# Early narrow products with sides exchanged, output weights split sooner, and adapter tables with the chunk index innermost

## The chip, the cores and the metric

One NeuronCore of a Trainium2 chip runs the kernel. Its engines have a row each in the profile: TensorE (PE, with its weight loads as PEld), VectorE (DVE), ScalarE (ACT), GpSimd (POOL), and SyncE (SP), which here only issues DMAs. The metric is device microseconds of one execution, the median of several.

## What is computed

A stream x of 32 sequences x 64 tokens x 512 channels, float32, passes four residual layers:

```python
x = x + attention(x)      # paged cache, window 256, 8 query heads, 4 key heads of 64
x = x + x @ w1[subject]   # one of eight 64 x 64 matrices, applied along the tokens of a batch
x = x + x @ W_base.T + ((x @ Wt.T) @ A2[a].T @ B2[a].T) @ Wp.T * scale2[a]
x = x + x @ W3.T + (x @ A3[b].T @ B3[b].T) * scale3[b]
```

Keys and queries are normalised and rotated; new keys and values go into the cache before it is read. The adapters have rank 16; there are 4 in the third layer and 8 in the fourth.

## The kernel before

Each engine's program is written out by hand, with semaphores between them; what an engine does, it does in the order of its own list. A tile is two batches (128 tokens), so there are 16 tiles; a step k of the main loop is one batch of attention (32 steps).

**Before the loop.** TensorE makes keys and values of all 16 tiles (`key_tile`, two per `key_pair`), which VectorE rotates and SP stores to `newkv`. Then it makes `queries(0)`, and from weights alone the folded matrices: the last two layers are linear, so they become one dense matrix `wf` and rank-32 terms per adapter pair. First come two narrow products of 512 x 512 weights with 64 columns: `wpt` with `b2` (called up, to `upt`) and `wt` with `a2` (to `t2tab`). `turned` makes each as 16 products with 128 columns of weights and 64 moving columns. Then `ct`, the product `t3` (`turned` with 128 moving columns, to `t3tab`), `u2f`, `queries_t(0)`, `keys_t(0)`, and `combined` and `fold` between the first `scores`. What is needed in two parts, a float32r high part and the rest, is copied by ScalarE (`..._high`, `evac`) and subtracted on VectorE (`low`, `..._low`): queries' and output weights through three `stage` buffers (`split_high`, `split_low` on POOL for the first four, `wo_low` for the last four). `root` on POOL is the power -1/2 of the norms; the gathers of cache rows are on the same queue.

**Tables.** `t2tab` and `t3tab` go to DRAM (`ttab2`, `ttab3`), and `load_tile` on SP fetches for each tile the four that its adapters need into `tsel`. In `ranks`, `tsel` is the weights' side of eight products with 128 moving columns, once for the high and once for the low part of x2:

```python
last = mm(sbk[2][:, 0:128], tsel[t % 2][:, c].rearrange("p v r -> p (v r)"), x2_s[a][:, c, :],
```

**The loop.** TensorE's even step: `keys_t` (transposes of cached keys), `queries(t+1)`, `probs_t` 0 and 1 (transposes of probabilities), `scores` of the next batch, `probs_t` 2 and 3, `project` (attention's output), `values`. Odd step: `keys_t`, `mix` (layer two of the tile before), `queries_t(t+1)` (transposes of the rotated query), `probs_t` 0 and 1, `scores`, `probs_t` 2 and 3, `base` and `ranks` (layers three and four), `values`, `up`. Bank `gb` is shared by `queries`, `project`, `mix` and `base`/`up`, so `queries` waits until ScalarE (`out_ev`) has emptied it. VectorE's even step: `attn_low`, `query_first`, four `soft` (mask and maximum of scores), `query_sums`, `scale(n, 0)`, `residual`, `query_last`, `scale(n, 1)`. Three batches of `newkv` and cache rows are gathered ahead.

Of the kernel before, what the change touches and what calls it, by code (L numbers as in the profile page):

```python
# [7 lines left out]
NB, NT, D = 32, 64, 512  # L8
# [67 lines left out]
def build(nc, xt, xtok, kvrows, wkv, wq, wo, qs, ks, w1, wbn, wt, a2t, b2t, wpt, s2, w3, a3t, b3t, s3,  # L76
# [4 lines left out]
    with ctx:  # L81
# [11 lines left out]
        ttab2 = nc.dram_tensor("ttab2", [NE2, 128, C, 2 * RANK], f32).ap()  # L93
        ttab3 = nc.dram_tensor("ttab3", [NE3, 128, C, 2 * RANK], f32).ap()
# [14 lines left out]
        t2tab = sb("t2tab", [128, NE2, C, 2, RANK], f32r)  # L109
        t3tab = sb("t3tab", [128, NE3, C, 2, RANK], f32r)  # L110
# [79 lines left out]
        def early(name, shape, dt=f32):  # L190
# [26 lines left out]
        tsel = [sb(f"tsel{i}", [128, C, 4, 2 * RANK], f32r) for i in range(2)]  # L217
# [12 lines left out]
            wb_ident w3_ident split_hi split_lo wo_lo up_mm up_ev t2_mm t2_hi t2_ev t3_mm t3_hi t3_ev ct_mm ct_ev u2f_mm u2f_ev u2_stored  # L230
# [17 lines left out]
        PAIRS = TILES // 2  # L248
        FOLD_BANKS = [ob, gb, tb[1], ob]
# [20 lines left out]
        def _(sp):  # L270
# [39 lines left out]
            for i in range(PAIRS):  # L310
                key_x(2 * i + 4)
                if i == 5:
                    spread_rows()
                key_x(2 * i + 5)
                for dst, src, name in pieces[i * each:(i + 1) * each]:
                    sp.dma_start(dst, src).then_inc(S[name], 16)
                if i >= 1:
                    store_pair(i - 1)
                if i == 2:
                    sp.wait_ge(S["split_lo"], 1)  # L320
                    load_split(3)
            store_pair(PAIRS - 1)
            for k in range(C, 2 * C):
                sp.wait_ge(S["split_lo"], min(k - 2, C))
                after(sp, S["wo_lo"], k - 2 - C)
                load_split(k)
# [11 lines left out]
            def load_tile(t):  # L338

                i = t % 2  # L340
                after(sp, S["x1_ready"], t)
                sp.dma_start(xtok_s[:], xtok[t]).then_inc(S["l_xtok"], 16)
                after(sp, S["l1_mm"], t - 1)
                for u in range(2):
                    s = sp.value_load(subj_s[0:1, 2 * t + u:2 * t + u + 1], min_val=0, max_val=7)
                    h = slice(64 * u, 64 * u + 64)
                    sp.dma_start(w1i[i][h, h], wtab[bass.ds(s, 1)].rearrange("a c n -> (a c) n")).then_inc(l_w1[i], 16)
                after(sp, S["out_mm"], t - 1)
                for u in range(2):
                    a2 = sp.value_load(ad2_s[0:1, 2 * t + u:2 * t + u + 1], min_val=0, max_val=NE2 - 1)  # L350
                    a3 = sp.value_load(ad3_s[0:1, 2 * t + u:2 * t + u + 1], min_val=0, max_val=NE3 - 1)
                    a23 = sp.value_load(pair_s[0:1, 2 * t + u:2 * t + u + 1], min_val=0, max_val=NE2 * NE3 - 1)
                    for l, tab, a in ((0, ttab2, a2), (1, ttab3, a3)):
                        sp.dma_start(tsel[i][:, :, 2 * u + l].bitcast(f32),
                                     tab[bass.ds(a, 1)].rearrange("a p c r -> (a p) c r")).then_inc(l_sel[i], 16)
                    sp.dma_start(usel[i][64 * u:64 * u + 32, :],
                                 utab2[bass.ds(a23, 1)].rearrange("a h r n -> (a h r) n")).then_inc(l_sel[i], 16)
                    sp.dma_start(usel[i][64 * u + 32:64 * u + 64, :],
                                 utab3[bass.ds(a3, 1)].rearrange("a h r n -> (a h r) n")).then_inc(l_sel[i], 16)
# [13 lines left out]
            sp.dma_start(ttab2.rearrange("e p c r -> p e (c r)"), t2tab[:].bitcast(f32).rearrange("p e c h r -> p e (c h r)")).then_inc(S["u_stored"], 16)  # L373
            sp.wait_ge(S["t3_ev"], 1)
            sp.dma_start(ttab3.rearrange("e p c r -> p e (c r)"), t3tab[:].bitcast(f32).rearrange("p e c h r -> p e (c h r)")).then_inc(S["u_stored"], 16)
# [27 lines left out]
        def _(pool):  # L403
# [57 lines left out]
            gather(0, 0)  # L461
            gather(1, 0)
            root("k", 7, 0)
            gather(2, 0)
            root("k", 8, 0)
# [22 lines left out]
        def _(act):  # L488
# [50 lines left out]
            for i in range(4, 7):  # L539
                key_pair(i)  # L540
            xq_high(0)
# [7 lines left out]

            query_square(0)  # L550
            split_high(4)
            evac(upt[:], bank[4][:, 0:256].rearrange("p (c r) -> p c r", c=C).unsqueeze(2).to_broadcast([128, C, 2, 64]), "up_mm", "up_ev")
            split_high(5)
            split_high(6)
            evac(t2tab[:, :, :, 0].rearrange("p e c r -> p c e r"), bank[5][:, 0:256].rearrange("p (c e r) -> p c e r", c=C, e=NE2), "t2_mm", "t2_hi")
# [47 lines left out]
            split_high(7)  # L603
            evac(t3tab[:, :, :, 0].rearrange("p e c r -> p c e r"), tb[1][:].rearrange("p (c e r) -> p c e r", c=C, e=NE3), "t3_mm", "t3_hi")
# [6 lines left out]
            for j in range(3):  # L611
                fold_high(j)
# [3 lines left out]
            for k in range(NB):  # L616
                t, n = k // 2, k + 1
                if k % 2 == 0:
                    if t >= 1:
                        attn_high(t - 1)  # L620
                    if t >= 2:
                        out_ev(t - 2)
                    if k > 0:
                        keys_ev(n)
                        if t + 1 < TILES:
                            query_square(t + 1)
                    probs_ev(k, 0)
                    probs_ev(k, 1)
                    exps(n, 0)
                    probs_ev(k, 2)  # L630
                    probs_ev(k, 3)
                    exps(n, 1)
                    exps(n, 2)
                    exps(n, 3)
                else:
                    if n < NB:
                        keys_ev(n)
                    if t >= 1:
                        mixed_high(t - 1)
                    if t + 1 < TILES:  # L640
                        queries_ev(t + 1)
                    probs_ev(k, 0)
                    probs_ev(k, 1)
                    if n < NB:
                        exps(n, 0)
                    probs_ev(k, 2)
                    probs_ev(k, 3)
                    if n < NB:
                        exps(n, 1)
                        exps(n, 2)  # L650
                    if t + 2 < TILES:
                        xq_high(t + 2)
                    if n < NB:
                        exps(n, 3)
# [7 lines left out]
        def _(dve):  # L662
# [165 lines left out]
            def wo_low(k):  # L828
# [6 lines left out]
            query_sums(0)  # L835
            wo_low(4)
            wo_low(5)
            low(t2tab[:, :, :, 0].rearrange("p e c r -> p c e r"), t2tab[:, :, :, 1].rearrange("p e c r -> p c e r"),
                bank[5][:, 0:256].rearrange("p (c e r) -> p c e r", c=C, e=NE2), "t2_hi", 1, "t2_ev")
            query_last(0)  # L840
            wo_low(6)
            xq_low(1)
            wo_low(7)
            low(t3tab[:, :, :, 0].rearrange("p e c r -> p c e r"), t3tab[:, :, :, 1].rearrange("p e c r -> p c e r"),
# [36 lines left out]
            def ranks(t):  # L881
                dve.wait_ge(S["z_mm"], t + 1)
                V.tensor_tensor(zm, sbk[2][:, 0:128], con("same_batch"), ALU.mult).then_inc(S["z_ready"], 1)
# [15 lines left out]
            scale(0, 1)  # L899
            combine(2)  # L900
# [6 lines left out]
            for k in range(NB):  # L907
                t, n = k // 2, k + 1
                if k % 2 == 0:
                    if t >= 1:  # L910
                        attn_low(t - 1)
                        if t + 1 < TILES:
                            query_first(t + 1)
                    else:
                        query_last(1)
                    for g in range(G):
                        soft(n, g)
                    if 0 < t < TILES - 1:
                        query_sums(t + 1)
                    scale(n, 0)  # L920
                    if t >= 1:
                        residual(t - 1)
                    if 0 < t < TILES - 1:
                        query_last(t + 1)
# [21 lines left out]
        def _(pe):  # L946
# [33 lines left out]
            def queries_t(t):  # L980
                pe.wait_ge(S["q_rot"], t + 1)
                after(pe, S["z_ready"], t - 2)
# [33 lines left out]
            pe.wait_ge(S["split_lo"], C)  # L1016
            queries(0)

# [5 lines left out]

            pe.wait_ge(S["l_wpt"], 16 * C)
            pe.wait_ge(S["l_low"], 32)
            pe.wait_ge(S["rows_ready"], 1)
            turned(bank[4], wpt_s, b2_s, 64).then_inc(S["up_mm"], 1)
            pe.wait_ge(S["l_wt"], 16 * C)
            turned(bank[5], wt_s, a2_s, 64).then_inc(S["t2_mm"], 1)  # L1030
# [39 lines left out]
            def scores(b):  # L1070
                t, u = b // 2, b % 2
                pe.wait_ge(S["qt_ev"], t + 1)
                if u == 0:
                    after(pe, S["z_ready"], t - 2)
# [46 lines left out]
            def ranks(t, b):  # L1121
                pe.wait_ge(l_sel[t % 2], 128 * (t // 2 + 1))
                pe.wait_ge(S["x2_lo"], t + 1)
                after(pe, S["negs_ready"], min(4 * b + 3, 4 * NB))
                for a in range(2):
                    for c in range(C):
                        last = mm(sbk[2][:, 0:128], tsel[t % 2][:, c].rearrange("p v r -> p (v r)"), x2_s[a][:, c, :],  # L1127
# [19 lines left out]
            for k in range(NB):  # L1147
# [18 lines left out]
                else:  # L1166
                    if t >= 1:
                        mix(t - 1)
# [3 lines left out]
                    probs_t(k, 1)  # L1172
                    if n < NB:
# [69 lines left out]
```

## Time and profile before

| what | us |
|---|---|
| median of 3 runs | 474.25 (472.82 to 475.46) |
| the profiled execution: time | 475.29 |
| its span, first to last instruction | 473.4 |
| mean granted clock of TensorE | 0.993 |
| busy: PE, DVE, ACT, POOL | 448.3, 277.2, 225.1, 260.0 |

The span is what the trace covers. Matmuls overlap in the pipeline, so their start-to-start distance, not their duration, tells what one costs. In a timeline, a bracket at the end of a row says how long the engine had been idle before it and what ended that.

### The profile page before, as it was taken

To read this page: it belongs to the slowest core of one execution; us is meant where nothing else is said; L and a number is where in the kernel's file an instruction comes from. 1 tells how busy PE (TensorE), PEld (TensorE's weight loads), DVE (VectorE), ACT (ScalarE), POOL (GpSimd) and SP (SyncE) were. 2 spreads that over 40 slices of the span, in tenths; PEclk is the share of its full clock that TensorE was granted. 3 is DMA by queue.
4 is the path that set the end of the run, shared out by engine and by line. 5 is a ranking of instruction groups with operands and counts; after the bars stand their busy time and mean duration, and the time that the engine had idled before them with its cause. 6 is when DMAs were issued, how large, how long until landed. Compare 5 with 4: busy or idle time off the path is not lost.

```text
span 473.4 us, 9807 instructions
## 1 busy us (share of the span) xinstructions
PE 448.3 (95%) x2847; PEld 320.8 (68%) x2847; DVE 277.2 (59%) x801; ACT 225.1 (48%) x600; POOL 260.0 (55%) x240
## 2 busy tenths in 40 slices
PE   5999997999989999999999999999999999999985
PEld 1434436745668777777777787877777777778763
DVE  2998867453666656464847466655646484746411
ACT  1331211352845564555647465556455564746521
POOL 3468176833355656666666565565666666654000
PEclk9999998999989999999999999999999999999999
DMA  7669676664444555556464636455554646352220
GB/s 227 212 201 310 208 256 191 182 201 129 114 124 105 161 128 152 133 153 152 128 164 116 173 104 169 110 148 133 154 142 128 160 131 159 95 156 71 72 70 22
DMA packets 81402, 70.34 MB, mean 149 GB/s; under 512 B 51684, under 2 KB 57700, under 8 KB 81350
## 3 DMA queue, kind: packets, MB, share of 16 engines
q1 hardware_dynamic: 64688, 47.23, 35.3%
q0 software_dynamic: 15456, 22.08, 17.0%
q10 hardware_dynamic: 1206, 0.42, 0.4%
q8 instruction: 23, 0.38, 0.3%
q14 instruction: 29, 0.24, 0.2%
HBM read 79.66 MB, written 11.93 MB: 193 GB/s over the span
## 4 chain that ended last, share of the span: by engine, by line
PE 76%; DVE 7%; ACT 5%; issue 5%; POOL 3%; DMA 3%; SPq 0%; ACTq 0%; POOLq 0%; DVEq 0%
PE bank L957 29%; PE bank L1099 9%; PE bank L1081 9%; PE bank L1087 7%; PE bank L951 4%; PE bank L1133 4%; PE bank L1114 3%; PE bank L970 3%; PE bank L1127 3%; PE bank L1066 3%; ACT w_late L595 2%; ACT qt_s L585 2%; POOL windows L454 2%; DMA cst<-const_dram 2%; DMA stage<-wo_dram 1%
## 5 line engine op out<-in xcount | busy, mean ns | idle before, releaser
L454 POOL DMA_INDIRECT windows<-kvrows_dram,idx_all x96 | 97.1, 1011 | 76.9 <-PE bank L1099 56.4
L454 POOL DMA_INDIRECT windows<-newkv,idx_all x96 | 96.3, 1003 | 35.9 <-issue 28.9
L567 ACT ACTIVATE prob<-prob,negmax 128x336 f32<-128x336 f32 x128 | 72.5, 570 | 30.7 <-DVE negmax L857 30.7
L427 POOL TENSOR_TENSOR rstd<-ms,half 128x8 f32<-128x8 f32 x24 | 46.4, 1932 | 47.6 <-DVE ms L796 28.9
L970 PE MATMUL bank<-wkv_s,xt_s 128*128 128x512 f32 x128 | 60.3, 629 | 6.5 <-DMA wkv_s<-wkv_dram 5.8
L857 DVE CUSTOM_DVE_ANT_0 prob<-bank,mask 128x336 f32<-128x336 f32 x128 | 57.2, 503 | 15.0 <-PE bank L1081 13.8
L573 ACT ACTIVATE pt_s<-bank 112x384 f32<-112x384 f32 x128 | 55.1, 485 | 0.3 <-PE bank L1087 0.3
L1087 PE MATMUL bank<-cst,prob 128*112 128x128 f32 x384 | 54.3, 278 | 0.5 <-ACT pt_s L573 0.5
L1087 PEld LDWEIGHTS bank<-cst,prob 128*112 128x112 f32 x384 | 42.4, 134 | 17.8 <-issue 15.9
L970 PEld LDWEIGHTS bank<-wkv_s,xt_s 128*128 128x128 f32 x128 | 25.0, 200 | 39.5 <-issue 36.9
L1099 PE MATMUL bank<-pt_s,windows 112*64 112x128 f32 x768 | 49.4, 277 | 0.3 <-ACT pt_s L573 0.3
L789 DVE TENSOR_TENSOR t<-bank,qcos 128x512 f32<-128x512 f32 x16 | 11.1, 692 | 61.1 <-ACT sq L548 61.1
L1099 PEld LDWEIGHTS bank<-pt_s,windows 112*64 112x64 f32 x768 | 41.2, 137 | 7.7 <-issue 5.8
L1081 PE MATMUL bank<-kt_s,qt_s 64*128 64x336 f32 x256 | 44.8, 468 | 1.5 <-issue 0.2
L867 DVE TENSOR_SCALAR prob<-prob,rinv 128x336 f32<-128x336 f32 x128 | 44.9, 393 | 2.3
L561 ACT ACTIVATE kt_s<-bank 128x336 f32<-128x336 f32 x64 | 25.3, 449 | 27.5 <-PE bank L1066 27.5
L957 PE MATMUL bank<-wq_hi,xq_hi 128*128 128x512 f32 x64 | 28.0, 437 | 8.7 <-DVE xq_lo L823 6.1
L1081 PEld LDWEIGHTS bank<-kt_s,qt_s 64*128 64x128 f32 x256 | 22.1, 186 | 14.4 <-ACT qt_s L585 5.0
L548 ACT ACTIVATE sq<-bank 128x512 f32<-128x512 f32 x16 | 9.6, 597 | 46.7 <-PE bank L957 46.7
L957 PE MATMUL bank<-wf_hi,x_hi 128*128 128x512 f32 x64 | 26.6, 415 | 1.4 <-DVE x_lo L823 1.4
L957 PE MATMUL bank<-wo_hi,ot_hi 128*128 128x512 f32 x64 | 26.5, 414 | 0.8 <-ACT w_late L595 0.8
L1066 PEld LDWEIGHTS bank<-cst,windows 112*128 112x128 f32 x192 | 20.0, 141 | 10.3 <-issue 6.6
(171 smaller groups left out, 772.2 us busy)
## 6 DMA issues: line engine op xcount, KB each, us to landing
xt_s<-xt_dram SPq DMA_DIRECT2D x32, 256.0 KB, 3.3
mask<-masks_dram SPq DMA_DIRECT2D x32, 168.0 KB
newkv<-kvo SPq DMA_DIRECT2D x16, 256.0 KB, 3.8
stage<-xtok_dram SPq DMA_DIRECT2D x16, 256.0 KB, 2.5
tsel<-ttab SPq DMA_DIRECT2D x64, 64.0 KB
out_dram<-w_late SPq DMA_DIRECT2D x16, 256.0 KB, 4.4
stage<-utab SPq DMA_DIRECT2D x32, 64.0 KB
wbn_late<-utab SPq DMA_DIRECT2D x32, 64.0 KB
```

Source lines behind the costliest of these rows:

```text
L427: P.tensor_tensor(rstd[i][:], ms[:], half[:], ALU.pow).then_inc(S[w + "_rstd"], 1)
L454: P.indirect_dma_start(kv_s[b % 4][:, c, :], None, newkv if new else kvrows, bass.IndirectOffsetOnAxis(ap=idx_all[:, new * CH + c, b:b + 1 ...
L567: A.activation(pr, pr, ACT.Exp, bias=negmax[:, g:g + 1], scale=-1.0, accum_out=psum_p[b % 2][:, g:g + 1]).then_inc(S["exp_done"], 1)
L573: A.activation(pt_s[g][:], tb[g % 2][0:KP, 0:CH * 128].rearrange("p (c q) -> p c q", c=CH), ACT.Copy).then_inc(S["pt_ev"], 1)
L857: V.tensor_tensor_reduce(out=prob[b % 3][:, g, :], in0=sbk[g][:, 0:WK], in1=mask[b % 3][:], scale=-1.0 / 16, scalar=3.0e38, op0=ALU.add, o ...
L867: V.tensor_scalar(pr, pr, rinv[b % 2][:, g:g + 1], None, ALU.mult).then_inc(S["norm_done"], 1)
L957: last = mm(to, lhs(a, c), rhs(b, c), start=(c == 0 and a == b), stop=(c == C - 1 and a == 1 and not more))
L970: last = mm(to[:], xt_s[n % 4][:, c, :], wkv_s[:, c, :], start=(c == 0), stop=(c == C - 1))
L1066: last = nc.tensor.transpose(sbk[p][:, KP * c:KP * c + KP], kv_s[b % 4][:, c, 128 * p:128 * p + 128], ident[0:KP, 0:KP])
L1081: mm(sbk[g][:, 0:WK], qt_s[t % 2][r, cols], kt_s[b % 2][p][r, :], start=True, stop=True).then_inc(S["s_mm"], 1)
L1087: last = nc.tensor.transpose(tb[g % 2][0:KP, 128 * c:128 * c + 128], prob[b % 3][:, g, KP * c:KP * c + KP], ident)
L1099: last = mm(ob[64 * h:64 * h + 64, col:col + 128], kv_s[b % 4][:, c, 256 + 64 * g:320 + 64 * g], pt_s[g][:, c, :], start=(c == 0), stop=(c ...
```

## The change

- The two narrow products are made together ahead of `queries(0)`: the 64-column side becomes the weights and the 512 x 512 side moves, up's in the lower and t2's in the upper 64 partitions of bank 4. ScalarE copies the result to `lows`, and TensorE turns it with four transposes into bank 5.
- Splits 4 and 5 (output weights) go up between the last key pairs on ScalarE, and the loads 4, 5 and 6 on SP up among the key tiles' loads; split 7 goes down behind `fold_high(0)`. Root 7 on POOL comes one gather earlier, and root 8 too.
- In the loop `mix` and `mixed_high` go behind the first two `probs_t` and `probs_ev`; on VectorE `query_sums` follows `query_first`, and `query_last` goes ahead of `residual`.
- `ranks` writes bank 0 instead of bank 2 and waits for the maxima of the first score group rather than of three; the waits of `queries_t` and `scores` on `z_ready` go.
- `t2tab`, `t3tab`, their DRAM tables and `tsel` have the chunk of 128 model columns (4 of them) as innermost index.

```diff
-        t2tab = sb("t2tab", [128, NE2, C, 2, RANK], f32r)
-        t3tab = sb("t3tab", [128, NE3, C, 2, RANK], f32r)
+        t2tab = sb("t2tab", [128, NE2, 2, RANK, C], f32r)
+        t3tab = sb("t3tab", [128, NE3, 2, RANK, C], f32r)
...
-        tsel = [sb(f"tsel{i}", [128, C, 4, 2 * RANK], f32r) for i in range(2)]
+        tsel = [sb(f"tsel{i}", [128, 4, 2 * RANK, C], f32r) for i in range(2)]
...
+        lows = u2c[3]
+        low_t = bank[5][:].rearrange("p (c r) -> p c r", c=C)
...
-                if i == 2:
-                    sp.wait_ge(S["split_lo"], 1)
-                    load_split(3)
+                k = {2: 3, 3: 4, 4: 5, 6: 6}.get(i, 0)
+                if k:
+                    sp.wait_ge(S["split_lo"], k - 2)
+                    load_split(k)
             store_pair(PAIRS - 1)
-            for k in range(C, 2 * C):
-                sp.wait_ge(S["split_lo"], min(k - 2, C))
-                after(sp, S["wo_lo"], k - 2 - C)
-                load_split(k)
+            sp.wait_ge(S["wo_lo"], 1)
+            load_split(7)
...
-                        sp.dma_start(tsel[i][:, :, 2 * u + l].bitcast(f32),
-                                     tab[bass.ds(a, 1)].rearrange("a p c r -> (a p) c r")).then_inc(l_sel[i], 16)
+                        sp.dma_start(tsel[i][:, 2 * u + l].bitcast(f32),
+                                     tab[bass.ds(a, 1)].rearrange("a p r c -> (a p) r c")).then_inc(l_sel[i], 16)
...
             gather(0, 0)
+            root("k", 7, 0)
             gather(1, 0)
-            root("k", 7, 0)
+            root("k", 8, 0)
             gather(2, 0)
-            root("k", 8, 0)
             root("q", 1, 1)
...
                 key_pair(i)
+                if i > 4:
+                    split_high(i - 1)
             xq_high(0)
...
+            evac(lows, bank[4][:], "low_mm", "low_ev")
             query_square(0)
-            split_high(4)
-            evac(upt[:], bank[4][:, 0:256].rearrange("p (c r) -> p c r", c=C).unsqueeze(2).to_broadcast([128, C, 2, 64]), "up_mm", "up_ev")
-            split_high(5)
+            evac(upt[:], low_t[:, :, 0:64].unsqueeze(2).to_broadcast([128, C, 2, 64]), "low_t", "up_ev")
+            evac(t2tab[:, :, 0].rearrange("p e r c -> p c e r"), low_t[:, :, 64:128].rearrange("p c (e r) -> p c e r", e=NE2), "low_t", "t2_hi")
             split_high(6)
-            evac(t2tab[:, :, :, 0].rearrange("p e c r -> p c e r"), bank[5][:, 0:256].rearrange("p (c e r) -> p c e r", c=C, e=NE2), "t2_mm", "t2_hi")
...
-            for j in range(3):
+            fold_high(0)
+            split_high(7)
+            for j in range(1, 3):
                 fold_high(j)
...
-                    if t >= 1:
-                        mixed_high(t - 1)
                     if t + 1 < TILES:
                         queries_ev(t + 1)
                     probs_ev(k, 0)
                     probs_ev(k, 1)
+                    if t >= 1:
+                        mixed_high(t - 1)
...
                         if t + 1 < TILES:
                             query_first(t + 1)
+                            query_sums(t + 1)
...
+                    scale(n, 0)
                     if 0 < t < TILES - 1:
-                        query_sums(t + 1)
-                    scale(n, 0)
+                        query_last(t + 1)
                     if t >= 1:
                         residual(t - 1)
-                    if 0 < t < TILES - 1:
-                        query_last(t + 1)
                     scale(n, 1)
...
-            turned(bank[4], wpt_s, b2_s, 64).then_inc(S["up_mm"], 1)
-            pe.wait_ge(S["l_wt"], 16 * C)
-            turned(bank[5], wt_s, a2_s, 64).then_inc(S["t2_mm"], 1)
+            for c in range(C):
+                for h, r, w in ((0, b2_s, wpt_s), (1, a2_s, wt_s)):
+                    last = mm(bank[4][64 * h:64 * h + 64, :], r[:, c, :], w[:, c, :], start=(c == 0), stop=(c == C - 1))
+            last.then_inc(S["low_mm"], 1)
+            pe.wait_ge(S["split_lo"], C)
+            queries(0)
+            pe.wait_ge(S["low_ev"], 1)
+            for c in range(C):
+                last = nc.tensor.transpose(low_t[:, c, :], lows[:, 128 * c:128 * c + 128], ident)
+            last.then_inc(S["low_t"], 1)
...
-                        last = mm(sbk[2][:, 0:128], tsel[t % 2][:, c].rearrange("p v r -> p (v r)"), x2_s[a][:, c, :],
+                        last = mm(sbk[0][:, 0:128], tsel[t % 2][:].rearrange("p v r c -> p (v r) c")[:, :, c], x2_s[a][:, c, :],
...
-                    if t >= 1:
-                        mix(t - 1)
                     if t + 1 < TILES:
                         queries_t(t + 1)
                     probs_t(k, 0)
                     probs_t(k, 1)
+                    if t >= 1:
+                        mix(t - 1)
```

## Rows read from the trace of the kernel before

**Rows 1.** The page: TensorE's busy time, and the chain that ended last.

```profile
PE 448.3 (95%) x2847; PEld 320.8 (68%) x2847; DVE 277.2 (59%) x801; ACT 225.1 (48%) x600; POOL 260.0 (55%) x240
...
PE 76%; DVE 7%; ACT 5%; issue 5%; POOL 3%; DMA 3%; SPq 0%; ACTq 0%; POOLq 0%; DVEq 0%
```

**Rows 2.** Busy time in one tile's period; last columns: clock, DMA share, GB/s.

```profile
287.23:309.21 21.98, 21.70 (x158) 16.93 (x159) 12.97 (x40) 12.58 (x35) 13.97 (x13) 1.00 0.55 142
```

**Rows 3.** Waits from 155 to 440 us: total, times, longest.

```profile
PEld bank L1066 <- DMA windows<-newkv,idx_all: 3.3, 12, 0.3
...
PEld bank L1081 <- ACT qt_s L585: 4.3, 13, 0.3
...
PE bank L957 <- ACT w_late L595: 2.6, 13, 0.2
PEld bank L1081 <- issue: 2.3, 13, 0.2
```

**Rows 4.** TensorE's timeline before the loop: start, duration, line, form.

```profile
74.31 0.47 PE L957 MATMUL bank<-wq_hi,xq_hi 128*128 128x512 f32 x1 [3.92 <-DVE xq_lo L823]
...
78.72 3.68 PE L951 MATMUL bank<-b_s,wpt_late 128*128 128x64 f32 x32
...
85.81 1.06 PE L951 MATMUL bank<-upt,a_s 128*128 128x64 f32 x8
87.88 3.81 PE L951 MATMUL bank<-a_s,wbn_late 128*128 128x128 f32 x32 [1.01 <-DVE t2tab L823]
...
94.96 0.60 PE L986 MATMUL bank<-cst,qrot 128*128 128x128 f32 x4
```

**Rows 5.** One microsecond within `queries(0)`, columns as in rows 2.

```profile
75.00:76.00 1.00, 1.00 (x5) 0.71 (x4) 1.00 (x6) 0.00 (x0) 0.70 (x2) 0.51 0.68 209
```

**Rows 6.** Timelines of POOL and VectorE before the loop.

```profile
69.95 1.68 POOL L427 TENSOR_TENSOR rstd<-ms,half 128x8 f32<-128x8 f32 x1
...
73.48 0.69 DVE L823 TENSOR_TENSOR xq_lo<-xt_s,xq_hi 128x512 fp32r<-128x512 f32 x1
...
79.61 0.69 DVE L789 TENSOR_TENSOR t<-bank,qcos 128x512 f32<-128x512 f32 x1 [0.86 <-ACT sq L548]
...
81.67 0.68 DVE L798 TENSOR_TENSOR t<-t 128x512 f32<-128x512 f32 x1
...
87.30 0.42 DVE L823 TENSOR_TENSOR t2tab<-bank,t2tab 128x256 fp32r<-128x256 f32 x1 [0.24 <-ACT t2tab L527]
```

**Rows 7.** Timelines of POOL's gathers and of a weight load behind one.

```profile
107.08 0.99 POOL L454 DMA_INDIRECT windows<-newkv,idx_all  x1 [7.00 <-DMA windows<-kvrows_dram,idx_all]
...
304.64 0.98 POOL L454 DMA_INDIRECT windows<-newkv,idx_all  x1 [0.30 <-issue]
...
307.84 0.14 PEld L1066 LDWEIGHTS bank<-cst,windows 112*128 112x128 f32 x1 [0.24 <-DMA windows<-newkv,idx_all]
```

**Rows 8.** The chain in order of time: start, us until the next, instructions.

```profile
104.55 6.87 PE bank L951 x16
...
144.09 0.92 PE bank L1114 x8
...
148.37 2.80 PE bank L957 x12
151.17 0.84 PE bank L1127 x8
152.01 1.46 PE bank L1099 x24
```

**Rows 9.** Timelines of VectorE and TensorE in the loop, and TensorE in step 31.

```profile
296.97 0.69 DVE L804 TENSOR_TENSOR qrot<-t,rstd 128x512 f32<-128x512 f32 x1 [0.22 <-issue]
...
297.20 0.79 PE L1066 MATMUL bank<-cst,windows 112*128 112x112 f32 x6
...
450.49 0.89 PE L1087 MATMUL bank<-cst,prob 128*112 128x128 f32 x6 [0.50 <-ACT pt_s L573]
```

**Rows 10.** Weight loads of `ranks` and of `values` by form: busy us, mean ns.

```profile
L1099 PEld LDWEIGHTS bank<-pt_s,windows 112*64 112x64 f32 x768 | 41.2, 137 | 7.7 <-issue 5.8 <-ACT pt_s L573 0.8
...
L1127 PEld LDWEIGHTS bank<-x_hi,tsel 128*128 128x128 f32 x64 | 9.6, 190 | 1.5
```

More of the change, by code:

```diff
@@ L92, in build @@
         utab3 = nc.dram_tensor("utab3", [NE3, 2, RANK, 512], f32).ap()
-        ttab2 = nc.dram_tensor("ttab2", [NE2, 128, C, 2 * RANK], f32).ap()
-        ttab3 = nc.dram_tensor("ttab3", [NE3, 128, C, 2 * RANK], f32).ap()
+        ttab2 = nc.dram_tensor("ttab2", [NE2, 128, 2 * RANK, C], f32).ap()
+        ttab3 = nc.dram_tensor("ttab3", [NE3, 128, 2 * RANK, C], f32).ap()
         wtab = nc.dram_tensor("wtab", [8, NT, NT], f32).ap()
@@ L229, in build @@
             ka_mm k_sq k_vc k_ss k_ms k_rstd k_t2 k_n k_rot
-            wb_ident w3_ident split_hi split_lo wo_lo up_mm up_ev t2_mm t2_hi t2_ev t3_mm t3_hi t3_ev ct_mm ct_ev u2f_mm u2f_ev u2_stored
+            wb_ident w3_ident split_hi split_lo wo_lo low_mm low_ev low_t up_ev t2_hi t2_ev t3_mm t3_hi t3_ev ct_mm ct_ev u2f_mm u2f_ev u2_stored
             b3_scaled comb_mm comb_ev wf_mm wf_hi wf_ev u_stored
@@ L372, in _ @@
             sp.wait_ge(S["t2_ev"], 1)
-            sp.dma_start(ttab2.rearrange("e p c r -> p e (c r)"), t2tab[:].bitcast(f32).rearrange("p e c h r -> p e (c h r)")).then_inc(S["u_stored"], 16)
+            sp.dma_start(ttab2.rearrange("e p r c -> p e (r c)"), t2tab[:].bitcast(f32).rearrange("p e h r c -> p e (h r c)")).then_inc(S["u_stored"], 16)
             sp.wait_ge(S["t3_ev"], 1)
-            sp.dma_start(ttab3.rearrange("e p c r -> p e (c r)"), t3tab[:].bitcast(f32).rearrange("p e c h r -> p e (c h r)")).then_inc(S["u_stored"], 16)
+            sp.dma_start(ttab3.rearrange("e p r c -> p e (r c)"), t3tab[:].bitcast(f32).rearrange("p e h r c -> p e (h r c)")).then_inc(S["u_stored"], 16)
             sp.wait_ge(S["b3_scaled"], 1)
@@ L602, in _ @@
             xq_high(1)
-            split_high(7)
-            evac(t3tab[:, :, :, 0].rearrange("p e c r -> p c e r"), tb[1][:].rearrange("p (c e r) -> p c e r", c=C, e=NE3), "t3_mm", "t3_hi")
+            evac(t3tab[:, :, 0].rearrange("p e r c -> p c e r"), tb[1][:].rearrange("p (c e r) -> p c e r", c=C, e=NE3), "t3_mm", "t3_hi")
             act.wait_ge(S["u2f_mm"], 1)
@@ L835, in _ @@
             query_sums(0)
+            low(t2tab[:, :, 0].rearrange("p e r c -> p c e r"), t2tab[:, :, 1].rearrange("p e r c -> p c e r"),
+                low_t[:, :, 64:128].rearrange("p c (e r) -> p c e r", e=NE2), "t2_hi", 1, "t2_ev")
             wo_low(4)
+            query_last(0)
             wo_low(5)
-            low(t2tab[:, :, :, 0].rearrange("p e c r -> p c e r"), t2tab[:, :, :, 1].rearrange("p e c r -> p c e r"),
-                bank[5][:, 0:256].rearrange("p (c e r) -> p c e r", c=C, e=NE2), "t2_hi", 1, "t2_ev")
-            query_last(0)
             wo_low(6)
             xq_low(1)
-            wo_low(7)
-            low(t3tab[:, :, :, 0].rearrange("p e c r -> p c e r"), t3tab[:, :, :, 1].rearrange("p e c r -> p c e r"),
+            low(t3tab[:, :, 0].rearrange("p e r c -> p c e r"), t3tab[:, :, 1].rearrange("p e r c -> p c e r"),
                 tb[1][:].rearrange("p (c e r) -> p c e r", c=C, e=NE3), "t3_hi", 1, "t3_ev")
@@ L882, in ranks @@
                 dve.wait_ge(S["z_mm"], t + 1)
-                V.tensor_tensor(zm, sbk[2][:, 0:128], con("same_batch"), ALU.mult).then_inc(S["z_ready"], 1)
+                V.tensor_tensor(zm, sbk[0][:, 0:128], con("same_batch"), ALU.mult).then_inc(S["z_ready"], 1)
             def fold_low(k):
@@ L899, in _ @@
             scale(0, 1)
+            wo_low(7)
             combine(2)
@@ L981, in queries_t @@
                 pe.wait_ge(S["q_rot"], t + 1)
-                after(pe, S["z_ready"], t - 2)
                 after(pe, S["negs_ready"], min(8 * t, 4 * NB))
@@ L1015, in _ @@
                 key_tile(n)
-            pe.wait_ge(S["split_lo"], C)
-            queries(0)
             def turned(to, w, r, n):
@@ L1026, in _ @@
             pe.wait_ge(S["l_low"], 32)
+            pe.wait_ge(S["l_wt"], 16 * C)
             pe.wait_ge(S["rows_ready"], 1)
-            turned(bank[4], wpt_s, b2_s, 64).then_inc(S["up_mm"], 1)
-            pe.wait_ge(S["l_wt"], 16 * C)
-            turned(bank[5], wt_s, a2_s, 64).then_inc(S["t2_mm"], 1)
+            for c in range(C):
[8 more added lines that the diff above has]
+            last.then_inc(S["low_t"], 1)
             pe.wait_ge(S["up_ev"], 1)
@@ L1072, in scores @@
                 pe.wait_ge(S["qt_ev"], t + 1)
-                if u == 0:
-                    after(pe, S["z_ready"], t - 2)
                 pe.wait_ge(S["kt_ev"], 2 * b + 2)
@@ L1123, in ranks @@
                 pe.wait_ge(S["x2_lo"], t + 1)
-                after(pe, S["negs_ready"], min(4 * b + 3, 4 * NB))
+                after(pe, S["negs_ready"], min(4 * b + 1, 4 * NB))
                 for a in range(2):
                     for c in range(C):
-                        last = mm(sbk[2][:, 0:128], tsel[t % 2][:, c].rearrange("p v r -> p (v r)"), x2_s[a][:, c, :],
+                        last = mm(sbk[0][:, 0:128], tsel[t % 2][:].rearrange("p v r c -> p (v r) c")[:, :, c], x2_s[a][:, c, :],
                                   start=(a == 0 and c == 0), stop=(a == 1 and c == C - 1))
```

## The prediction

> **What bounds the kernel now.** I read the page first: TensorE is busy 95% of the span and the chain that ended last is 76% TensorE [rows 1]. So a part is worth only what it gives to TensorE's row. Two regions have different limits.
>
> The loop over the tiles repeats every 21.98 us with full clock and 21.70 us of TensorE busy [rows 2]. The waits of the loop say what is left to win: per tile 0.33 us of weight load ahead of the odd step's scores (ACT's `qt_s`), 0.2 us ahead of `queries` for `out_ev`, and some 0.28 us ahead of `keys_t` for a gather [rows 3]. The last two lie in one place: after `up`, the bank must be evacuated, and `keys_t` is done meanwhile. They are untouched.
>
> The time before the loop (to about 118 us) has the real holes. In TensorE's timeline, `queries(0)` starts at 74.31 after 3.92 us of idleness, so the key tiles ended at 70.39; the two narrow products take 78.72 to 85.81, and `t3` starts at 87.88 after another 1.01 us for VectorE's half of `t2tab` [rows 4]. After the long hole the granted clock is 0.51 [rows 5], the 1.2 GHz level of the two, and `queries(0)` takes 78.72 - 74.31 = 4.41 us.
>
> **The early part, step by step.** Root 7 on POOL starts at 69.95, behind six gathers; `xq_lo` ends at 73.48 + 0.69 = 74.17, which is what `queries(0)` waited for [rows 6]. The change puts the root ahead of the second three gathers, each 0.98 + 0.30 us [rows 7]: 3.85 us earlier, so `xq_lo` is ready at 70.3. Gathers 1 and 2 come later, but their keys are first transposed long after this.
>
> TensorE now does the narrow products at 70.39. Before, they are 64 matmul instructions of 64 columns in 85.81 - 78.72 = 7.09 us. After, they are 8 float32 products with 64 columns of weights and 512 moving columns, two instructions each: 16. An instruction of 512 float32 columns costs 6.87 / 16 = 0.43 us, so 6.9 us one after another. But they alternate between the two halves of the output partitions, as the value products at L1099 do: those cost 1.46 / 24 = 0.061 us, against 0.92 / 8 = 0.115 us at L1114, whose weights fill the array and which move the same 128 columns [rows 8]. By that ratio, 0.53, the 16 cost 3.65 us. I take that (it is the same form) and keep 6.9 as the other end. Their inputs are loaded while the key tiles run, so nothing else holds them. They end at 74.05.
>
> `queries(0)` then costs the 2.80 us of 12 such matmuls at full clock [rows 8]: to 76.85. The hole is filled and the slow clock with it. Four transposes add 0.43 us (77.3); ScalarE's evacuation of `lows` runs beside `queries(0)`. ScalarE then does the square and `upt` (0.6 us each): `ct` can start at 78.3 and, at 87.88 - 1.01 - 85.81 = 1.06 us [rows 4], ends at 79.4. `t3` needs `t2_ev`. VectorE's query step started 79.61 - 78.72 = 0.89 us after `queries(0)` ended [rows 4, 6], so now at 77.75; its six instructions take 2.74 us (79.61 to the end of the add at 81.67 + 0.68 = 82.35), and the low half of `t2tab` 0.42 us more [rows 6]: 80.9. So `t3` starts at 80.95 instead of 87.88: 6.9 us earlier. The table is now written with 16 bytes between elements. Nothing in the trace shows such a write; below it may be nothing, above, twice the 0.42 us; I use 6.8 us.
>
> The two holes left, 1.0 and 1.5 us, could lower the clock: 1.01 us did not in the old trace, 3.92 did. I take nothing, and 1.5 us (half of the 3 us following) as the other end.
>
> The splits of the output weights lose nothing: ScalarE's copies of 0.6 us move into its idle time between key pairs, and SP issues their loads among those of the key tiles, of which each is asked for three key tiles ahead of its use. Split 7 now comes after the loop's first exponentials; it puts 0.6 us ahead of `combine(2)` on VectorE, and `fold(2)`, which waits for `comb_ev`, starts 6.87 / 2 = 3.4 us after `fold(1)`: just covered.
>
> After `t3`, TensorE is dense to `queries_t(0)`: 94.96 - 87.88 = 7.08 us [rows 4], now 88.0, and `keys_t(0)` follows four transposes later at 88.5. That needs the gather of new rows of batch 0. This gained less: its root waits for the query's `ms` (79.7), 1.7 to 2 us of root, three gathers of 1.3: issued by 85.9, only 2 us sooner than before. In the loop such a gather ended issuing at 304.64 + 0.98 = 305.62 and was waited for until 307.84, 2.2 us [rows 7]; that gives 88.1, hidden. But the gather of 3, issued by 107.08 - 7.00 = 100.08, took 7.0 us to land [rows 7]. I take 0 because in the new order only masks are ahead of it (four 256 KB weight loads were, before).
>
> **The loop.** `mix(t-1)` goes behind `probs_t(k, 1)`, with its copy on ScalarE, so that `queries_ev` and two copies of probabilities are done while `mix` runs. What goes is the 0.33 us load wait, less the 0.18 us that the same load shows as issue in the other half [rows 3]: 0.15 to 0.33, I take 0.2, for 14 tiles: 2.8 us. In step 31 TensorE waited 0.50 us for `pt_s` behind the same copy [rows 9]: gone.
>
> Two things must not become late. First `queries_t`, which now starts right behind `keys_t`'s six transposes: near 297.20 + 6 x 0.105 = 297.83 (a transpose moves 112 columns and has the pitch of the `ranks` matmuls). `qrot` was done at 296.97 + 0.69 = 297.66 [rows 9]. In the new order `query_sums` (1.5 us, the last three of the six instructions above) stands ahead of `soft`, so `negmax` and the exponentials come 1.4 us later; `scale(n, 0)`, which stood behind the sums anyway, ends 0.8 us later, near 297.0, while the root, whose input comes 1.7 us sooner, no longer holds anything. `query_last` then ends at 297.7. It fits by 0.1 us. `residual` follows, done at 298.4; `mix` asks for it ten transposes after 297.83, at 298.9. `scale(n, 1)` ends 0.6 us later and is read a step of `scores` after that.
>
> Second, `mixed_low` now sits ahead of `soft(n, 0)`, which starts about 0.2 us later than before; `mix` ends at 298.9 + 0.92 = 299.8, the copy and the subtraction (0.6 and 0.7 us, with 0.2 of latency) end at 301.3, and `base`, behind `scores` and two `probs_t` (2 us), asks for `x2_lo` at 301.8. What is queued behind it on VectorE, the next exponentials' maxima, is needed by ScalarE 0.2 us later too; nothing of the next step waits on them within 2 us. The loads on SP that wait for `x1_ready` begin 1.4 us later, and are for the tile after.
>
> **The tables with 16 bytes between weights.** The transfers fall from 512 pieces of 128 bytes to 128 of 512 bytes each; no wait on them is in the path, so nothing. The price is on TensorE: `ranks` reads `tsel` as weights, 8 loads per tile, 128 in all. A load of 128 columns is 190 ns, one of 64 columns 137 ns [rows 10]: 0.8 ns per column. Adjacent `ranks` matmuls lie 0.84 / 8 = 0.105 us apart [rows 8]: here the load, not the 128 columns that move, sets the pace, and nothing would hide a slower one. No row has a strided load. Below: nothing. Above: each column costs twice, 0.107 us per load, 13.7 us in all. I take nothing, because the dense products move a column each 0.23 / 512 = 0.45 ns, so the memory serves elements at nearly twice the pace that a load asks of it.
>
> The Trainium skill (Advanced Engine Details and Errata, SBUF Cachelines) speaks against this: lines are of 16 bytes, two accesses on a line are needed for full pace, and one line per access is penalised. Taken as twice the time per load, an estimate, that rule gives the time of rival 1, the rows' pace argument 464.5; no row of this kernel tests it, since none has such a stride.
>
> **Sum.** 6.8 + 2.8 + 0.5 = 10.1 us. The profiled execution took 475.29 us (span 473.4), 1.0 above the median of 474.25; taken off the median that is 464.15, with a little for the thin margins 464.5.
>
> **Rivals.** (1) Strided weight loads at half pace: 464.5 + 13.7 = 478.2, slower. It decides from 10.1 / 128 = 79 ns per load. For: that load has no cover; against: the pace argument. 0.17; half of that penalty, 471.4, 0.07. (2) The gather of batch 0 lands as late as that of 3: 4.3 us of waiting and a slow clock behind it, 1.5: 470.3; 0.08. (3) The column halves don't overlap: 3.25 us of it come back, 467.8; 0.05. (4) The thin margins of the loop fail: `queries_t` or `mix` waits as long as the scores did: 2.8 to 5 us back, 468.5; 0.07. My forecast: 0.56.
>
> A measurement of this kernel tells 0.5% (2.4 us) from no change. Slower is rival 1: 0.16. The same are parts of the half penalty and of several costs together: 0.08. Faster 0.76. The range runs from 460.5 (both loop ends at their best, and gathers eased by the bigger pieces) to 474, leaving out rival 1.
>
> **What would show it.** `queries(0)` directly behind the narrow products near 74 us, without slow clock; 16 instructions there in 3.7 us; `t3` at 81 and `keys_t(0)` at 88.6; a tile period of 21.8 us without the wait for `qt_s`. The `ranks` loads at 190 ns and the eight in 0.84 us: if they take 1.5 us or more, rival 1 has it and I am wrong in sign.

## The result, and the profile after

The changed kernel takes 481.57 us (median of 4), the kernel before 473.91 beside it: a ratio of 1.0143, 95% interval 1.0102 to 1.0183. It is slower; 464.5 and "faster" were predicted. The profiled execution took 481.42 us, its span 479.5, against 475.29 and 473.4: 6.1 us to explain from the two traces. The medians lie 7.7 us apart, because the traced execution of the kernel before was 1.4 us above its median here.

The page after, first its sums and the chain (they answer to [rows 1]):

```profile
PE 457.4 (95%) x2803; PEld 329.6 (69%) x2803; DVE 276.1 (58%) x801; ACT 226.7 (47%) x601; POOL 255.1 (53%) x240
...
PE 81%; DVE 5%; issue 5%; ACT 3%; POOL 3%; DMA 2%; ACTq 0%; POOLq 0%; DVEq 0%
```

TensorE has 44 instructions fewer and is busy 9 us longer. A longer row on the engine that sets the pace, with less in it, says that some instruction became dearer. First the part ahead of the loop, TensorE's timeline (against [rows 4]):

```profile
70.58 0.64 PE L1030 MATMUL bank<-wpt_late,b_s 128*64 128x512 f32 x1
70.59 0.64 PE L1030 MATMUL bank<-wt_s,a_s 128*64 128x512 f32 x1
...
73.64 0.59 PE L1030 MATMUL bank<-wt_s,a_s 128*64 128x512 f32 x1
74.16 0.50 PE L959 MATMUL bank<-wq_hi,xq_hi 128*128 128x512 f32 x1
...
77.03 0.60 PE L1036 MATMUL bank<-cst,prob 128*128 128x128 f32 x4
78.36 1.10 PE L953 MATMUL bank<-upt,a_s 128*128 128x64 f32 x8 [0.74 <-ACT upt L528]
81.32 3.81 PE L953 MATMUL bank<-a_s,wbn_late 128*128 128x128 f32 x32 [1.85 <-DVE t2tab L826]
...
88.40 0.60 PE L987 MATMUL bank<-cst,qrot 128*128 128x128 f32 x4
89.76 0.79 PE L1073 MATMUL bank<-cst,windows 112*128 112x112 f32 x6 [0.75 <-DMA windows<-newkv,idx_all]
```

The narrow products run in pairs, one for each half of the output partitions, from 70.58 to 74.16 in the old hole. `queries(0)` takes 77.03 - 74.16 = 2.87 us with a granted clock of 1.00, and `keys_t(0)` comes at 89.76 instead of 95.39: 5.6 us are gained there. Now one tile's period (against [rows 2]), and the loop's waits (against [rows 3]):

```profile
286.56:309.25 22.69, 22.49 (x159) 17.90 (x159) 12.94 (x40) 12.63 (x35) 13.61 (x13) 1.00 0.47 137
```

```profile
PE bank L959 <- ACT w_late L597: 2.4, 12, 0.2
PEld bank L1086 <- issue: 2.1, 12, 0.2
PEld bank L1138 <- issue: 2.1, 12, 0.2
PEld bank L1073 <- DMA windows<-newkv,idx_all: 0.2, 1, 0.2
```

The wait of the scores' weights for `qt_s` is gone, and the waits for gathers too, yet a period takes 22.69 instead of 21.98 us. The chain and the groups by form show where (against [rows 8] and [rows 10]):

```profile
142.64 2.81 PE bank L959 x12
145.45 1.70 PE bank L1132 x8
147.15 1.46 PE bank L1104 x24
```

```profile
L1132 PEld LDWEIGHTS bank<-x_lo,tsel 128*128 128x128 f32 x64 | 16.5, 330 | 0.0
L1132 PEld LDWEIGHTS bank<-x_hi,tsel 128*128 128x128 f32 x64 | 16.2, 321 | 0.7
```

The eight loads and matmuls of `ranks` take 1.70 instead of 0.84 us, a load 320 to 330 ns instead of 190. The pieces beside them in this stretch of the chain are as long as before. The account: 16 x 0.86 = 13.8 us lost, 5.6 gained ahead of the loop, 14 x (0.86 - 0.71) = 2.1 gained by the loop's order, together 6.1 us more, the difference of the spans.

### The profile page after: what moved, and what is told of

It reads as the page before. It is cut to its first block, busy times and chain, and to the rows that moved or that the text cites. A ratio compares the mean times of both kernels' runs of the same rounds, so it can differ in the third digit from the quotient of the medians.

```text
span 479.5 us, 9707 instructions
## 1 busy us (share of the span) xinstructions
PE 457.4 (95%) x2803; PEld 329.6 (69%) x2803; DVE 276.1 (58%) x801; ACT 226.7 (47%) x601; POOL 255.1 (53%) x240
## 2 busy tenths in 40 slices
DMA packets 56826, 70.34 MB, mean 147 GB/s; under 512 B 18916, under 2 KB 33124, under 8 KB 56774
## 4 chain that ended last, share of the span: by engine, by line
PE 81%; DVE 5%; issue 5%; ACT 3%; POOL 3%; DMA 2%; ACTq 0%; POOLq 0%; DVEq 0%
PE bank L959 29%; PE bank L1104 9%; PE bank L1092 9%; PE bank L1086 9%; PE bank L1132 6%; PE bank L972 5%; PE bank L1138 4%; PE bank L1119 3%; PE bank L953 3%; PE bank L1073 3%; POOL windows L455 2%; ACT w_late L597 2%; DMA cst<-const_dram 1%; PE bank L987 1%; ACT prob L569 1%
## 5 line engine op out<-in xcount | busy, mean ns | idle before, releaser
L428 POOL TENSOR_TENSOR rstd<-ms,half 128x8 f32<-128x8 f32 x24 | 41.1, 1714 | 26.4 <-DVE ms L725 20.5
L581 ACT ACTIVATE ot_hi<-bank 128x512 fp32r<-128x512 f32 x16 | 9.5, 596 | 44.8 <-PE bank L1104 44.8
```

The costliest lines, as they stand in the source:

```text
L428: P.tensor_tensor(rstd[i][:], ms[:], half[:], ALU.pow).then_inc(S[w + "_rstd"], 1)
```

## The experiments

**The tables alone, undone and alone.** Theory: weights 16 bytes apart. Rivals: what else changed around `ranks`, its bank and its place.

```diff
 # undo_tables: the changed kernel with the layout of before; only_tables: the reverse on the kernel before
-        tsel = [sb(f"tsel{i}", [128, 4, 2 * RANK, C], f32r) for i in range(2)]
+        tsel = [sb(f"tsel{i}", [128, C, 4, 2 * RANK], f32r) for i in range(2)]
...
```

undo_tables:

> The changed kernel with the tables and tsel laid out as before (weights side by side), all else of the change kept. Theory (weights 16 bytes apart load at half pace): ranks is back at 190 ns per load and 0.84 us per tile, the tile period falls from 22.69 to about 21.83 us, and 16 x 0.86 = 13.7 us come off, with some 0.6 us of the faster table writes: about 467.3 us. Rival (the new bank, the new order of mix, or the earlier wait in ranks slow it): ranks stays near 1.70 us and the time near 481 us. Rival (the size of the DMA pieces): the same 467, but with loads of 320 ns still there and the gain in waits.

only_tables:

> The kernel before with nothing but the tables and tsel laid out as in the change. Theory (stride of the weights): 16 x 0.86 = 13.7 us more, plus under 1 us for the strided table writes ahead of t3: about 488 us, loads of 320 to 330 ns. Rival (the order of the loop or the bank makes ranks slow): 474 us, as before.

Measured: undo_tables 469.44 us, ratio to the kernel before 0.9882 (0.9839 to 0.9926); only_tables 489.06 us, 1.0284 (1.0227 to 1.0342). The loads by form, first of undo_tables, then of only_tables:

```profile
L1132 PEld LDWEIGHTS bank<-x_hi,tsel 128*128 128x128 f32 x64 | 9.6, 190 | 1.5
```

```profile
L1127 PEld LDWEIGHTS bank<-x_hi,tsel 128*128 128x128 f32 x64 | 16.3, 321 | 0.8
```

The layout carries its price into the old kernel and takes it out of the new one, with the bank and the order of the loop as they were in each. The layout costs 12 us taken out of the new kernel (481.57 - 469.44) and 15 us put into the old one (489.06 - 474.08). All else of the change gains about 5: 474.08 - 469.44 = 4.6 by the medians. undo_tables lies 2.1 us above the 467.3 expected: by the two traces `ranks` gave back its 13.8 us and the part ahead of the loop 0.3, but the 12 matmuls of the last `base` took 1.5 us longer than in the changed kernel (4.60 instead of 3.07), with a granted clock of 0.63 there.

**How the price depends on the distance.** Pairs of chunks innermost (8 bytes), 12 bytes, 32 bytes, and the moving side instead of the weights.

```diff
 # pair
+        tsel = [sb(f"tsel{i}", [128, 2, 4, 2 * RANK, 2], f32r) for i in range(2)]
+   ... tsel[t % 2][:, c // 2].rearrange("p v r b -> p (v r) b")[:, :, c % 2]
 # stride3
+   ... tsel[t % 2][:].rearrange("p c v r -> p (c v r)")[:, 0:384:3]
 # stride8
+   ... wf_s[0][:].rearrange("p c n -> p (c n)")[:, 0:1024:8]
 # moving4, in base
+   ... lambda p, c: wf_s[p][:].rearrange("p c n -> p (c n)")[:, c:2048:4]
```

> The changed kernel with pairs of chunks innermost: weights 8 bytes apart instead of 16, pieces of 256 bytes. If the price is one 16-byte line per weight (two weights share a line here), loads take 190 ns and the time is that of undo_tables within 1 us, about 467.5 us. If any gap between weights halves the pace, loads take 320 ns and it is 481 us. In between, loads of about 255 ns and 474 us.

> undo_tables, but ranks takes its 128 weights 12 bytes apart from the same tile (128 of the first 384 elements), so the adapters' term is computed from the wrong weights; for its time alone. If the price is that of a line of 16 bytes per weight, three in four weights still open a new line: loads near 290 ns and the eight of ranks in some 1.5 us. If gaps up to 8 bytes are free and all above cost alike: 320 to 330 ns, 1.70 us. If only weights exactly a line apart pay: 195 ns.

> undo_tables, but ranks takes its weights 32 bytes apart from the folded matrix, so the adapters' term is wrong; for its time alone. If each weight pays for one line, as at 16 bytes: 320 to 330 ns per load, 1.70 us for the eight. If the price grows with the distance: 450 ns or more, 2.5 us.

> undo_tables, but the dense product of layers three and four (base) moves 512 columns that lie 16 bytes apart, so its result is wrong; for its time alone. My argument in the prediction was that the memory serves elements every 0.45 ns. If a line of 16 bytes per element costs the moving side as much as the weights' (about 1.66 ns per weight), the 12 matmuls of base take 12 x 512 x 1.66 = 10.2 us instead of 2.8, and the time grows by some 118 us. If the moving side is not touched, base stays at 2.8 us.

Pair took 469.11 us, ratio 0.9877 (0.9836 to 0.9918), as undo_tables. The other three were executed once each, on a chip that is no match for the first (below), so only the durations of their instructions are read. stride3 and stride8 keep the transfers of undo_tables, with pieces of 128 bytes; so the slow loads there don't come from the size of the pieces, the rival that undo_tables alone left open. Loads by form of pair, stride3 and stride8:

```profile
L1136 PEld LDWEIGHTS bank<-x_hi,tsel 128*128 128x128 f32 x64 | 10.0, 195 | 1.4
```

```profile
L1132 PEld LDWEIGHTS bank<-x_hi,tsel 128*128 128x128 f32 x64 | 13.4, 257 | 0.7
```

```profile
L1132 PEld LDWEIGHTS bank<-x_hi,wf_hi 128*128 128x128 f32 x64 | 16.6, 327 | 0.7
```

Their chains, the eight of `ranks` in stride3, then in stride8, and the 12 of `base` with those of `ranks` in moving4:

```profile
487.37 1.28 PE bank L1132 x8
```

```profile
437.41 1.74 PE bank L1132 x8
```

```profile
225.42 5.52 PE bank L959 x12
230.94 0.84 PE bank L1132 x8
```

| bytes between weights | us for the eight | ratio |
|---|---|---|
| 4 | 0.84 | 1 |
| 8 | 0.88 | 1.05 |
| 12 | 1.28 | 1.52 |
| 16 | 1.70 | 2.02 |
| 32 | 1.74 | 2.07 |

The price doesn't grow beyond 16 bytes, so it isn't the distance. It fits lines of 16 bytes: let a line cost the time of two weights at least, however few of its own are wanted. At 8 bytes each line gives two, nothing is lost; at 12 bytes four weights lie on three lines, six slots for four, 1.5; from 16 bytes on, 2. The measured ratios are these. My expectation for 12 bytes (1.5 us) counted a new line as a full price each time and was too high. That the two slots are the cause is a model that fits four ratios, not a thing that a trace shows. The Trainium skill (Advanced Engine Details and Errata, SBUF Cachelines) has the rule without a price: lines of 16 bytes, of which each needs at least two hits, else there is a penalty. The runs agree: hardly a price with two weights on a line (1.05), twice the time with one (2.02 and 2.07).

The moving side pays as well: `base` takes 5.52 (in other tiles up to 5.78) instead of 2.80 us, 0.90 ns a column instead of 0.46, at a granted clock of 1.00. I had expected either nothing or the weights' 1.66 ns; it is again half its own pace. The time of moving4, 528.69 us, doesn't show the 16 x 2.72 = 43.5 us that this adds to TensorE's work: on the same chip stride3 took 528.72, with TensorE busy 467.6 us (89% of the span) against 493.7 (94%) here. So idle time of TensorE took in a part of it; the rest wasn't followed up.

**The order of the loop.** early_only puts the loop's order back; loop_only has it alone, on the kernel before.

> undo_tables without the new order in the loop (mix, mixed_high, query_sums and query_last where they were; ranks in bank 0 as in the change). Theory: the part ahead of the loop keeps its 5.6 us, the loop has the old period of 21.98 us: about 468.8 us, 1.5 to 2.1 us above undo_tables. Rival (the loop's order gives nothing, or costs): equal to or below undo_tables.

> The kernel before with nothing but the new order in the loop: mix and mixed_high behind the first probs_t and probs_ev, query_sums up, query_last ahead of residual. 14 tiles x 0.15 us (period 21.83 instead of 21.98) and 0.5 us in step 31: about 2.6 us less, 471.4 us. Rival (the gain needs the early part, or is eaten by the gathers that keys_t waits for): under 1 us.

> loop_only once more: on the chip of its first run the kernel before took 521 us instead of 474, with pauses of 3 to 5 us of the engines that no wait explains, so it said nothing of 0.15 us per tile. Theory: where the kernel before takes some 474 us, 2.6 us less (period 21.83 instead of 21.98, 0.5 us in step 31). If the chip again shows those pauses: slower than before by some 3%, as in the first run, because the new order has less slack between engines.

> loop_only a third time. Where the kernel before takes some 474 us: 2.6 us less. With the pauses: 2 to 4% slower than the kernel before, as in both runs so far.

early_only took 469.81 us, ratio 0.9893 (0.9851 to 0.9935), beside undo_tables' 469.44. loop_only_3 took 474.82 us, ratio 0.9994 (0.9968 to 1.002). Yet its tile has the shorter period (against [rows 2]):

```profile
285.12:306.96 21.84, 21.64 (x158) 16.98 (x159) 12.94 (x40) 12.63 (x35) 13.62 (x13) 1.00 0.58 146
```

So the 0.15 us per tile are there, some 2.1 us in all. The 0.5 us of step 31 are not. The chain from the last `project` to the `base` of step 31, of the kernel before and of loop_only_3:

```profile
443.97 2.81 PE bank L957 x12
...
449.86 0.49 ACT pt_s L573
...
451.39 2.82 PE bank L957 x12
```

```profile
440.81 2.80 PE bank L956 x12
...
445.87 0.91 PE bank L1113 x8
...
446.80 0.61 ACT x_hi L590
...
447.43 0.70 DVE x_lo L823
...
448.18 3.07 PE bank L956 x12
```

That is 7.42 and 7.37 us. The wait for `pt_s` is gone, but `mix` now comes so late that `base` waits for its copy and its subtraction: the last step has no `scores` to cover them. The changed kernel has 7.38.

Of the 2.1 us the medians show nothing. In this one execution the clock gave and took in two places. The last `base` stands in the chain with 4.54 us, where the kernel before has 3.08, with a low granted clock (last columns as in [rows 2]):

```profile
461.79:466.33 4.54, 4.54 (x14) 3.63 (x15) 0.00 (x0) 0.00 (x0) 0.00 (x0) 0.64 0.00 0
```

The other place is `queries(2)`: 3.03 us at a clock of 1.00, where the kernel before has 4.36 us at 0.65, behind the same 2.17 us of idleness. undo_tables has the slow last `base` too (4.60 us); the changed kernel, early_only, pair and xq_early_3 don't (3.07), though all but early_only have the new order. So the order doesn't force it. The mean granted clock was 0.989 or less in 10 of the 12 executions of loop_only_3 and in 7 of the 17 of the kernel before beside it; whether a slow `base` at the end is behind that, and eats the 2.1 us, stays open.

**The hole that was left.** Ahead of `queries(2)` the kernel before, the changed one, undo_tables, only_tables, pair and early_only have 2.17 us of idleness and 4.4 to 4.6 us for its 12 matmuls; loop_only_3 has the same idleness and 3.03 us. The split of tile 2's x came last in step 1; its input had long been there.

```diff
             query_square(1)
+            xq_high(2)
             keys_ev(1)
...
             query_sums(1)
+            xq_low(2)
             fold_low(3)
...
-                    if t + 2 < TILES:
+                    if 2 < t + 2 < TILES:
```

> undo_tables with the split of tile 2's x (xq_high, xq_low) ahead of the loop instead of at the end of step 1. TensorE's last hole of over 2 us, ahead of queries(2), and the slow clock behind it go: 2.17 + (4.60 - 2.80) = 4.0 us less, about 465.4 us. Rival: something else is late by the same amount (the keys of batch 3, or project), and only the hole moves: under 1 us.

> xq_early once more, for the same reason. Where the kernel before takes some 474 us: 465.4 us, queries(2) directly behind keys_t(3) and its 12 matmuls in 2.8 instead of 4.6 us. Rival: the hole only moves, 468 to 469 us.

> undo_tables once more beside the two, as their reference on the same chip. Theory (its first run): 0.988 of the kernel before. On a chip with the pauses: the early part still gives its 5.6 us, but the order of the loop may cost more than that.

> xq_early a third time, in the hope of a chip without the pauses. Where the kernel before takes some 474 us: 465.4 us, queries(2) directly behind keys_t(3), its 12 matmuls in 2.8 instead of 4.6 us. Rival: the hole only moves, 468 to 469 us. With the pauses: within 0.5% of undo_tables, as in the second run.

xq_early_3, on a chip where the kernel before took 474.76 us, took 464.51 us, ratio 0.9807 (0.9765 to 0.9849), the best of all kernels here. TensorE's timeline of it:

```profile
122.35 0.79 PE L1075 MATMUL bank<-cst,windows 112*128 112x112 f32 x6
122.91 0.48 PE L961 MATMUL bank<-wq_hi,xq_hi 128*128 128x512 f32 x1
```

No idle time stands ahead of the second row, and the chain has 2.77 us for the 12, where undo_tables has 4.60. undo_tables did not run on this chip, so the gain is read across two chips, each against its kernel before: 0.9882 to 0.9807, some 3.6 us, where 4.0 were expected.

**The gather of batch 0.** gather_first moves that gather ahead of the query's root on POOL, and `query_last(0)` behind the splits on VectorE.

> xq_early with the gather of batch 0's new rows ahead of the first query's root on POOL (and query_last(0) behind the splits on VectorE). keys_t(0) waited 1.27 us for this gather in undo_tables: that goes, 1.2 us below xq_early. Rival: the stores of the last keys have not landed by then, and POOL waits with the root behind it: no gain.

In its timeline `keys_t(0)` follows `queries_t(0)` without a wait:

```profile
88.78 0.60 PE L989 MATMUL bank<-cst,qrot 128*128 128x128 f32 x4
89.22 0.74 PE L1075 MATMUL bank<-cst,windows 112*128 112x112 f32 x6
```

That shows no gain. xq_early_2, without the move, has no wait there either and starts `keys_t(0)` at 89.31; in undo_tables it starts at 89.42 and in xq_early_3 at 88.90, both with the wait (1.27 and 1.46 us). The wait is missing where `queries_t(0)` came later (88.78 in gather_first and 88.88 in xq_early_2, against 87.55 and 86.85), and `keys_t(0)` starts where it did. On POOL the gather waited 1.44 us for the stores of the last keys, with the root behind it: the rival. On a chip like the first, gather_first did not run.

**Chips that pause.** The first runs of stride3, stride8, moving4, xq_early, loop_only and gather_first, and all of the second runs, fell on two chips where the kernel before took 521 to 535 us. In the traces from there, which are of the other kernels, ScalarE and VectorE pause again and again for some 3 to 5 us, and the profile names no instruction of this kernel that they wait for ("remote" stands for another core or an unknown queue, "issue" for none); of undo_tables_2, waits from 155 to 500 us:

```profile
ACT pt_s L575 <- remote: 50.4, 15, 4.7
DVE t L792 <- issue: 39.5, 8, 6.1
```

| kernel | us | kernel before beside it | ratio |
|---|---|---|---|
| xq_early | 530.54 | 521.4 | unclear: 518.2 to 535.33 against 511.53 to 533.74 |
| xq_early_2 | 540.14 | 535.51 | 1.0208 (1.0085 to 1.0331) |
| undo_tables_2 | 540.26 | 535.51 | 1.0245 (1.0126 to 1.0364) |
| loop_only | 538.69 | 521.27 | 1.0325 (1.0229 to 1.0421) |
| loop_only_2 | 550.23 | 535.51 | 1.0432 (1.0346 to 1.0519) |
| gather_first | 528.13 | 521.27 | 1.0142 (1.0083 to 1.0201) |

But for the first run of xq_early, whose executions overlap with those of the kernel before, all kernels of the table are slower there than the kernel before, undo_tables too, which is 1.2% faster elsewhere; loop_only, which differs by the order alone, loses most. So on these chips the order costs 3 to 4%. Why the pauses come, and through which wait the order makes them dearer, stays open.

## Why the prediction was wrong

**The step that failed** is "I take nothing, because the dense products move a column each 0.23 / 512 = 0.45 ns, so the memory serves elements at nearly twice the pace that a load asks of it". The argument compared elements that lie side by side with elements that don't, as if the pace were that of the memory. moving4 shows that it isn't: at 16 bytes the moving side falls to half its own pace. The upper bound stood beside it, 13.7 us, with the right reason (nothing covers a slower load): measured 16 x 0.86 = 13.8 us. Rival 1 had the place, the mechanism and the price, and 0.17 of the chance (0.16 where the chances are summed). Its 478.2 us lies 3.4 us below the 481.57 measured, because the other terms brought less than their 10.1 us. The rule of the Trainium skill (Advanced Engine Details and Errata, SBUF Cachelines) stood against the choice, and I overruled it with an inference where only a measurement of a stride could have.

**Ahead of the loop** the mechanism was right: 3.58 us for the narrow products (3.65 expected from the ratio at L1099), a clock of 1.00 in `queries(0)`, `t3` at 81.32 (80.95). The strided write of the table cost more than nothing: ScalarE's part of `t2tab` 0.65 instead of 0.36 us, VectorE's 0.60 instead of 0.42. The gather of batch 0, taken as hidden, held `keys_t(0)` for 0.75 us, rival 2 in small. Its three parts took 1.46, 1.45 and 0.99 us on POOL, so the last was issued at 86.89 instead of 85.9, and `keys_t(0)` could start 2.9 us after that, at 89.76, instead of 2.2. Term 6.8, measured 5.6.

**The loop's order** was sized right in the trace (0.2 per tile taken, 0.15 measured, the `qt_s` wait gone) and both margins held. The 0.5 us of step 31 failed: the wait moved from `pt_s` to `base`, and 0.05 us are left. 2.8 + 0.5 us were taken, 2.1 + 0.05 stand in the traces. In the times stand 0.4 (early_only less undo_tables) and nothing (loop_only_3), and on chips that pause the order costs.

**The transfers** were a term of nothing and are: under 512 bytes there are 18916 packets instead of 51684, and the gathers no longer held `keys_t` in the loop, but the period is set elsewhere. In undo_tables, with small pieces and the shorter period, that wait was 8.3 us over 12 tiles, inside the time in which `out_ev` empties the bank.

## What to carry to other kernels

Before a layout is changed for its DMAs, look at who reads it as weights and how far apart. Here float32r weights 8 bytes apart kept the pace (0.88 against 0.84 us for eight loads), 12 bytes cost half as much again, 16 and 32 bytes the double; and where the load sets the pace of small matmuls, nothing hides that. Pairs of chunks keep the pace and still halve the number of pieces. Where an unknown cost has no cover and its upper end decides the sign, an argument by analogy isn't enough to put it at its lower end. A reorder that wins tenths of a microsecond per tile may bring nothing in the median, and here it lost 3 to 4% on chips whose engines pause. And where a wait is moved, look at the last step too: what covers it elsewhere may be missing there.

## What the runs showed of the hardware that I had not expected

- Weights at 4, 8, 12, 16 and 32 bytes: 0.84, 0.88, 1.28, 1.70, 1.74 us for eight of 128 columns; moving columns at 16 bytes: 0.90 instead of 0.46 ns each.
- Writes with 16 bytes between float32r elements: ScalarE 1.08 instead of 0.60 us for 128x512, VectorE (which also reads the high half so) 1.10 instead of 0.69.
- The same 2.17 us of idleness ahead of `queries(2)` was followed by a granted clock of 0.65 in the kernel before (4.36 us for 12 matmuls) and of 1.00 in loop_only_3 (3.03 us).
- The kernel before takes 474 us on two chips and 521 to 535 on two others. The mean granted clock was 0.978 to 0.996 on the former (one execution of 887 us left aside) and 0.947 to 0.989 on the latter, too small a difference for 10 to 13%.
